# Flamingo layer, one core: the values' product and the output projection one step later, all middle probabilities turned by VectorE

## What is computed

```python
q = rmsnorm(layernorm(x) @ Wq.T)            # 32 heads of 128
k, v = rmsnorm(ctx @ Wk.T), ctx @ Wv.T      # 8 heads of 128, 4 query heads share one
probs = softmax(q @ k.T / sqrt(128) + mask) # 64 x 64 for each sequence and head
x = x + tanh(g_xattn) * ((probs @ v) @ Wo.T)
x = x + tanh(g_ffn) * experts_and_shared(layernorm(x))
```

## Time and profile before

| what | value |
|---|---|
| median of 3 launches (lowest, highest) | 1366.54 us (1366.28, 1366.75) |
| the profiled execution: device time | 1367.91 us |
| the profiled execution: span of the core | 1366.2 us |
| TensorE busy | 1351.8 us, 99% |
| VectorE busy | 1041.6 us, 76% |
| ScalarE busy | 505.4 us, 37% |
| GpSimd busy | 359.9 us, 26% |
| mean granted TensorE clock | 0.999 |

### The profile page before, as it was taken

One profiled execution on the slowest core, in us unless ns is written; L12 is line 12 of the kernel. 1 busy time (PEld: TensorE's weight loads), 2 busy tenths in 40 slices (PEclk: granted clock), 3 DMA queues, 4 the chain that ended last, 5 costly groups with the idle time before them and its releaser, 6 DMA issues.

```text
span 1366.2 us, 24589 instructions
## 1 busy us (share of the span) xinstructions
PE 1351.8 (99%) x8473; PEld 1092.8 (80%) x8474; DVE 1041.6 (76%) x2190; ACT 505.4 (37%) x1085; POOL 359.9 (26%) x375
## 2 busy tenths in 40 slices
PE   8999999999999999999999999999999999999998
PEld 7888877888888888888888888888887888777777
DVE  6676668898888888898988888888687655334459
ACT  4233244343434444344334343434344321222242
POOL 1122232212121221212121212122112100467746
PEclk9999999999999999999999999999999999999999
DMA  6766631222122221222121222212222344555548
GB/s 208 248 190 204 187 112 40 59 56 72 50 57 66 62 59 47 76 53 59 50 78 48 59 63 66 55 51 59 55 78 85 132 171 161 193 185 162 168 158 297
DMA packets 178209, 146.13 MB, mean 107 GB/s; under 512 B 77376, under 2 KB 139328, under 8 KB 177856
## 3 DMA queue, kind: packets, MB, share of 16 engines
q1 hardware_dynamic: 170592, 120.17, 29.4%
q0 software_dynamic: 7520, 24.65, 5.4%
HBM read 97.06 MB, written 47.71 MB: 106 GB/s over the span
## 4 chain that ended last, share of the span: by engine, by line
PE 80%; DVE 3%; issue 1%; DMA 0%; ACT 0%; POOL 0%; DVEq 0%; ACTq 0%
PE ps L677 20%; PE ps L679 19%; PE ps L678 19%; PE ps L1071 6%; PE ps L761 5%; PE ps L808 4%; PE ps L1087 3%; PE ps L1066 2%; PE ps L793 1%; DVE acc L2086 1%; DVE acc L2093 1%; PE ps L984 1%; PE ps L816 0%; PE ps L1118 0%; PE ps L769 0%
## 5 line engine op out<-in xcount | busy, mean ns | idle before, releaser
L574 POOL CAST vth<-vt 128x256 fp32r<-128x256 f32 x64 | 25.4, 397 | 538.6 <-PE ps L808 536.6
L1268 ACT CAST ah<-ps 128x256 fp32r<-128x256 f32 x256 | 83.1, 381 | 208.4 <-PE ps L679 202.0
L677 PE MATMUL ps<-hT,w0h 128*128 128x512 f32 x384 | 152.2, 396 | 1.2 <-DVE w0l L1542 1.2
L679 PE MATMUL ps<-hT,w0h 128*128 128x512 f32 x384 | 149.8, 390 | 0.0
L678 PE MATMUL ps<-hT,w0l 128*128 128x512 f32 x384 | 149.6, 390 | 0.0
L568 POOL TENSOR_TENSOR qr<-qv,mhalf 128x8 f32<-128x8 f32 x64 | 105.1, 1642 | 139.2 <-DVE qv L1672 113.5
L1228 ACT ACTIVATE qs<-ps,wqk 128x512 f32<-128x512 f32 x128 | 88.2, 689 | 125.8 <-PE ps L679 125.8
L1623 DVE TENSOR_TENSOR acc<-ps,acc 128x512 f32<-128x512 f32 x128 | 88.0, 687 | 50.5 <-PE ps L679 50.3
L677 PE MATMUL ps<-w0l,ah 128*128 128x512 f32 x256 | 105.9, 414 | 0.0
L1241 ACT ACTIVATE pb<-pb 128x256 f32<-128x256 f32 x128 | 48.3, 419 | 154.4 <-DVE pb L1692 154.4
L677 PE MATMUL ps<-w1l,ah 128*128 128x512 f32 x256 | 105.1, 411 | 0.0
(11 more groups left out here) (255 smaller groups left out, 3172.8 us busy)
## 6 DMA issues: line engine op xcount, KB each, us to landing
wraw<-in_w_att SPq DMA_DIRECT2D x64, 256.0 KB, 2.7
vbuf<-vo SPq DMA_DIRECT2D x16, 512.0 KB, 3.3
kbuf<-ko SPq DMA_DIRECT2D x16, 512.0 KB, 5.3
kt<-kbuf SPq DMA_DIRECT2D x128, 64.0 KB, 2.2
vt<-vbuf SPq DMA_DIRECT2D x64, 128.0 KB, 2.2
wgu<-in_w_gu SPq DMA_DIRECT2D x4, 2048.0 KB, 7.9
y<-ybuf SPq DMA_DIRECT2D x16, 512.0 KB, 6.9
pbuf<-pbT SPq DMA_DIRECT2D x26, 256.0 KB, 2.0
```

Source lines behind the costliest of these rows:

```text
L677: pe.matmul(dst, l_hi, r_lo, start=first, stop=False)
L679: return pe.matmul(dst, l_hi, r_hi, start=False, stop=last)
L1268: act.copy(ah[:, bp, :, b2, :], pv_view(bp, b2)).then_inc(a_hi, 1)
```

## The change

- The values' product and both halves of the output projection come one step later: TensorE's step i now handles index i-2 (`probs_v(i - 2)`, `project_out` of i-3 and i-2), and ScalarE's and VectorE's parts for them move with it (`a_hi_tile(i - 2)`, `a_rest(i - 2)`, `add_out(2 * i - 3)`).
- The probabilities of all steps 2 to 56 take VectorE's transposition and the way over `pbuf`. TensorE's transposes remain at steps 0, 1 and 57 to 63. The rounding and the subtraction of an even step come one step later, those of an odd step at the end of its own step.
- At step 56 (`catch_up`) both index 54 and index 55 are handled, and from step 57 on the old order stands (`last_step`).
- The query sums of step 3 go through `q_sums` in place of `add_quarters` (`TURNED`).
- GpSimd's split of the values comes one step later, behind the inverse root of the step before.
- SyncE's loop is written out: in every middle step the store of `pbT` (`probs_out`) comes first, in odd steps then `load_k`, weight slice, `probs_back`, values; in even steps `probs_back`, values, weight slice.
- The low part of an odd weight slice stays last in VectorE's odd step, that of an even slice stays between the two turned squares of the odd step.

```diff
@@ -50,8 +50,8 @@
 NC = T // CT
 CB = CT // S
 STEPS = KVH * NC
-BY_DMA = (4, STEPS - NC)
-TURNED = (3, STEPS - NC + 1)
+BY_DMA = (2, STEPS - NC + 1)
+TURNED = (4, STEPS - NC + 1)
 E, EI = 16, 128
...
-            def next_loads(d, odd, x_tiles=(), k=None):
-
-                i = 2 * d + odd
-                if k is not None:
-                    sp.wait_ge(p_turned, k + 1)
-                    sp.wait_ge(p_back, 64 * k + 64)
-                    sp.dma_start(pbuf, pbT[:].rearrange("p c m i -> p c (m i)")).then_inc(p_out, 16)
-                if odd:
-                    sp.wait_ge(s_done, i + 1)
-                    load_k(d + 1)
...
-                    sp.wait_ge(v_split, 2 * i + 2)
-                    sp.dma_start(vt[:].rearrange("p b t -> p (b t)"), vbuf[i + 1]).then_inc(vt_in, 16)
+            def load_v(j):
+                sp.wait_ge(v_split, 2 * j)
+                sp.dma_start(vt[:].rearrange("p b t -> p (b t)"), vbuf[j]).then_inc(vt_in, 16)
+
+            def load_slice(i):
                 sp.wait_ge(w_hi, i + 8)
                 sp.wait_ge(w_lo, i + 8)
                 sp.dma_start(wraw[:], w_att[i + NC]).then_inc(wr_in, 16)
-                for n in x_tiles:
+
+            def probs_out(i):
+                sp.wait_ge(p_turned, i - BY_DMA[0] + 1)
+                if i > BY_DMA[0]:
+                    sp.wait_ge(p_back, 64 * (i - BY_DMA[0]))
+                sp.dma_start(pbuf, pbT[:].rearrange("p c m i -> p c (m i)")).then_inc(p_out, 16)
+
+            def probs_back(i):
+                sp.wait_ge(p_out, 16 * (i - BY_DMA[0] + 1))
+                sp.wait_ge(pT_evac, 2 * i)
+                for c in range(4):
+                    sp.dma_start(pt_raw[32 * c:32 * c + 32].rearrange("p q m i -> p q (m i)"),
+                                 p_ld[c]).then_inc(p_back, 16)
...
+            for i in range(STEPS - NC + 1):
+                if by_dma(i):
+                    probs_out(i)
+                if i % 2:
+                    sp.wait_ge(s_done, i + 1)
+                    load_k(i // 2 + 1)
+                if i == 0:
+                    load_v(1)
+                if i % 2 or not by_dma(i):
+                    load_slice(i)
+                if by_dma(i):
+                    probs_back(i)
+                    load_v(i)
+                if i % 2 == 0 and by_dma(i):
+                    load_slice(i)
+            load_v(STEPS - NC + 1)
+
+            for t in range(1, NC - 1):
+                i = STEPS - NC + t
+                if t % 2:
+                    sp.wait_ge(s_done, i + 1)
+                    load_k(i // 2 + 1)
...
             split_v(1)
-            split_v(2)
-            with pool.Fori(3, STEPS - 2) as j:
+            inverse_root(3)
+            with pool.Fori(4, STEPS - NC + 2) as j:
+                split_v(j - 2)
+                inverse_root(j)
+            split_v(STEPS - NC)
+            split_v(STEPS - NC + 1)
...
+            def next_query(i):
+                if i % NC == NC - 1:
+                    pe.wait_ge(w_lo, i + 5)
+                for h in range(2):
+                    pe.wait_ge(q_sq, 2 * i + 1 + h)
+                    q_head(h, (i + 1) % 2, (i + 1) % NC // 2, att(i + 1)).then_inc(q_done, 1)
+
+            def step(i):
+
+                next_query(i)
+                probs_v(i - 2, i % 2)
+                scores((i + 1) // 2, (i + 1) % 2)
+                pe.wait_ge(acc_done, 2 * (i - 2) + 1)
+                project_out(1, att(i - 3), (0, 1))
+                if i + 1 == TURNED[0]:
+                    pe.wait_ge(const_dve, 6)
+                add_quarters(i + 1)
+                project_out(1, att(i - 3), (2, 3))
+                if i % NC == 2:
+                    pe.wait_ge(w_lo, i + 6)
+                projected_0(i - 2, att(i - 2))
+
...
+            def catch_up(i):
+
+                next_query(i)
+                probs_v(i - 2, 0)
+                scores((i + 1) // 2, (i + 1) % 2)
+                q_sums(i + 1)
+                pe.wait_ge(acc_done, 2 * (i - 2) + 1)
+                project_out(1, att(i - 3), (0, 1, 2, 3))
+                projected_0(i - 2, att(i - 2))
+                probs_v(i - 1, 1)
+                pe.wait_ge(acc_done, 2 * (i - 1) + 1)
+                project_out(1, att(i - 2), (0, 1, 2, 3))
+                projected_0(i - 1, att(i - 1))
+
...
-                probs_v(1, 1)
                 pe.wait_ge(s_scaled, 3)
                 pe.wait_ge(ss_turned, 3)
...
-                pe.wait_ge(const_dve, 6)
-                pe.wait_ge(acc_done, 4)
-                transpose_probs(2, 0)
-                outputs(1, W[0], W[0])
-                step(1, 1, 2, W[0], W[0], W[0])
-
...
-            group((STEPS - NC) // 2, 1, last=True)
+                q_sums(3)
+
+            opening()
+            for i in range(3, STEPS - NC):
+                step(i)
+            catch_up(STEPS - NC)
+            for i in range(STEPS - NC + 1, STEPS - 1):
+                last_step(i, o_ready=STEPS if i == STEPS - NC + 1 else None, last=(i == STEPS - 2))
 
             r = STEPS - 2
...
+            def probs_hi(i, odd, bank=2):
+                if by_dma(i):
+                    act.wait_ge(p_back, 64 * (i - BY_DMA[0] + 1))
+                    act.wait_ge(pv_done, 2 * i + 2 - 2 * odd)
+                    act.copy(raw_view(0, odd), pt_raw[:]).then_inc(pT_hi, 2)
...
+            def act_step(i):
+
+                queries(i)
+                a_hi_tile(i - 2, 0)
+                if i % 2:
+                    probs_hi(i - 1, 0)
+                a_hi_tile(i - 2, 1)
+                split_slice(i, att(i + NC), i % NC)
+                if i % 2:
+                    probs_hi(i, 1)
+                exps(i + 1)
+
...
             def probs_lo(i, odd, bank=2):
-                if odd:
+                if by_dma(i):
+                    dve.wait_ge(pT_hi, 2 * i + 2)
+                    dve.tensor_tensor(raw_view(1, odd), pt_raw[:], raw_view(0, odd), ALU.subtract).then_inc(pT_evac, 2)
...
+            def turn_probs(i):
+                dve.wait_ge(p_ready, 2 * i + 2)
+                if i > BY_DMA[0]:
+                    dve.wait_ge(p_out, 16 * (i - BY_DMA[0]))
+                dve.transpose(pbT[:].rearrange("p c m i -> p (c m i)"),
+                              pb[:].rearrange("p (m z) (h j) -> p (z h) m j", z=2, h=2)).then_inc(p_turned, 1)
+
+            def dve_step(i):
+
+                odd = i % 2
+                turn_probs(i)
+                turn_squares(i + 1, 0)
+                sum_squares(i + 1, 0)
+                if odd:
+                    slice_lo(i - 1, att(i + NC), i % NC - 1)
+                turn_squares(i + 1, 1)
+                sum_squares(i + 1, 1)
+                split_sums(i + 1)
+                a_rest(i - 2, 0)
+
+                def while_root():
+                    if odd:
+                        probs_lo(i - 1, 0)
+                    add_out(2 * i - 3, 1, (2 * i - 5) % NT)
+                    a_rest(i - 2, 1)
+
+                def while_exp():
+                    add_out(2 * i - 2, 0, (2 * i - 4) % NT)
+
+                softmax(i + 1, while_root, while_exp, turn_before=i - BY_DMA[0] + 1)
                 if odd:
                     probs_lo(i, 1)
...
+                    slice_lo(i, att(i + NC), i % NC)
+
+            def dve_catch_up(i):
+
+                turn_probs(i)
+                a_rest(i - 2, 0)
+
+                def while_root():
+                    add_out(2 * i - 3, 1, (2 * i - 5) % NT)
+                    a_rest(i - 2, 1)
+
+                def while_exp():
+                    add_out(2 * i - 2, 0, (2 * i - 4) % NT)
+
+                softmax(i + 1, while_root, while_exp, turn_before=i - BY_DMA[0] + 1)
+                slice_lo(i, att(i + NC), i % NC)
+                a_rest(i - 1, 0)
+                add_out(2 * i - 1, 1, (2 * i - 3) % NT)
+                a_rest(i - 1, 1)
+                probs_lo(i, 0)
+                add_out(2 * i, 0, (2 * i - 2) % NT)
```

More of the change, by code:

```diff
@@ L305, in rows_by_pe, with by_dma, pT_before, att @@
             return isinstance(n, int) and (n < 2 or n == NT - 1)
[L307 to L317, removed]
+        def by_dma(i):
+            return BY_DMA[0] <= i < BY_DMA[1]
+        def pT_before(i):
+            return i if i < BY_DMA[0] else i - (BY_DMA[1] - BY_DMA[0])
+        def att(r):
+            return W[r // NC % 2]
+        def raw_view(x_, odd):
+            return pt[x_][:, :, odd * P:odd * P + P].rearrange("p m (q i) -> p q m i", q=4)
         def turned(j):
@@ L434, in next_loads @@
                     sp.dma_start(xt3[n % 2][:], x[n]).then_inc(x3_in[n % 2], 16)
[L435 to L458, removed]
+                load_v(i + 1)
             def store_h2(n):
@@ L826, in gate_up_half, with projected_0 @@
                     mm.then_inc(gu_done, 1)
[L828 to L837, removed]
+            def projected_0(r, w_o):
                 pe.wait_ge(a_hi, 4 * r + 6)
@@ L841, in outputs @@
                 project_out(0, w_o, (0, 1, 2, 3))
[L843 to L848, removed]
```

(52 more changed lines are left out.)

143 lines of the change are left out of this document (41 added, 102 removed).

## The result

| | median us | lowest, highest | launches |
|---|---|---|---|
| before | 1366.41 | 1365.63, 1366.75 | 4 |
| after | 1493.02 | 1492.11, 1493.88 | 4 |

The ratio is 1.0927, with a 95% interval of 1.0908 to 1.0946: slower by 127 us. The prediction had said 1437 with a range of 1421 to 1470, so the direction was right and the time too low by 56 us. The profiled execution of after took 1492.87 us, with a span of 1491.1.

What follows compares the result with a forecast made beforehand. TensorE, 99% busy, was taken as the bound, so delays reaching it cost full length. -13.0 +72.8 +2.6 -0.6 +7.6 +1.5 = +70.9 us on 1367.9 gives 1438.8, as launch median 1437 us; range 1421 to 1470.

Steps and rivals of the forecast that it cites:

- The transposes, -0.48 us each time: TensorE's steps without transposes: each four removed save 0.48 us, the difference of two neighbouring steps; -13.0 us in the sum.
- the rival with 18 us: TensorE's transposes cost their durations, 1.1 us for four: 18 us lower, 1419 us; chance 0.05.
- The keys behind a wait, 26 x 2.8 = +72.8 us: SyncE's odd steps: key loads queue behind the store awaiting VectorE's transposition, so TensorE waits 2.8 us before the scores.
- The clock, "I take no fall there": TensorE behind each odd step's 2.8 us wait: no clock fall after 26 us of dense work, 0 us.
- The rival stood there: TensorE's clock falls behind each wait: 0 to 39 us more, 1440 to 1476 us; chance 0.25.
- The way back and the split sums, +2.6 and 0: Odd steps: late return of probabilities delays VectorE, 0.1 x 26 = 2.6 us; VectorE's later split sum of squares costs 0.
- The bound for the first (8 us): Upper bound for the probabilities' way back in odd steps: 8 us, where 2.6 was taken.
- the bound of 0.1 a pair for the second: Upper bound for VectorE's late split sum of squares: 0.1 us a pair, where 0 was taken.
- The even steps' slice, "hidden with over 1 us to spare": Even steps: weight slice lands by 12.6 us, its rounding precedes the exponentials at 14.60, so no cost.
- Ends, -0.6 and +7.6: Both ends: scores after step 3's wait at 238.3 against 238.88, -0.6 us; step 56 takes back moved work, +7.6 us.
- "nearly 7": TensorE's idle time in step 3, nearly 7 us, with a clock fall behind it counted once as +1.5 us.
- The "faster" rival: SyncE's odd-step queue: keys come in time, TensorE stays the bound, 1354 us; chance 0.05.

Runs made afterwards that it cites:

- k_rests: `k_hi` with the odd slice's low part moved into VectorE's root wait of the next even step, and even slices rounded behind the exponentials: 1361.12 us.
- k_first_turns: `k_first` plus four TensorE transposes of an identity, read by nobody, ahead of the values' product in each odd step: 1379.55 us.
- k_first: The changed kernel with SyncE issuing an odd step's four key loads ahead of the store of the turned probabilities: 1371.72 us.
- fill6: The changed kernel with six useless matmuls of 512 columns ahead of the odd steps' scores: 1449.25 us.
- fill3: The changed kernel with three useless matmuls of 512 columns ahead of the odd steps' scores: 1476.03 us in one launch.
- k_hi: `k_first` with ScalarE rounding an odd step's returned probabilities behind the next exponentials, not ahead of them: 1366.26 us.
- k_slice: `k_first` with an even step's weight slice loaded ahead of the four loads of the probabilities, not behind them: 1369.65 us.

## Why the prediction was wrong

- **The transposes, -0.48 us each time.** Right in size on TensorE: 0.45 a pair in `k_rests`. In `k_first_turns` they cost 0.18 a pair, 0.29 by the medians, since VectorE hides a part. The durations as a price (the rival with 18 us) are refuted by both. The sentence from the Trainium skill's page "TensorE: Matmul & The Clock Gate", Part 4, gives a duration; taken as time on the path it would have been off by a factor of over two.
- **The keys behind a wait, 26 x 2.8 = +72.8 us.** Right: 75.4, 2.90 each. The worked step from the softmax's end over transposition, store and loads to the scores has 5.33 us, and 5.41 is the mean in after, measured from the transposition's start. That is partly luck, for two of its parts were off and cancelled: the first key load follows the store by 0.37 us, not 0.67, and from its issue to the scores it is 4.3 us, not 3.8. `k_first` shows that it is the order in the queue and not the loads.
- **The clock, "I take no fall there".** This is the step that failed. Each of the 26 waits lowered the clock, at 1.5 us each in 21 cases and 2.7 us in five: 45 us where the sum had 0. The rival stood there, with chance 0.25 and a bound of 1.5 each (39 us in all), and was what happened; even its top, 1476, was 17 us too low, because five falls cost more than its bound and other terms were short too. The argument against it was that over 26 us of dense matmuls lay between the waits, and that in the earlier trace rows the gaps lay close together. No row of before had a lone gap of this length, so the dense work around it was an argument without a row. The rows that were there (gaps of 1.16 and 1.94 us, clock 0.83) spoke for the fall, and the runs agree with them: gaps like the first did nothing in `fill6`, and the second lies where the clock starts to fall in `fill3`.
- **The way back and the split sums, +2.6 and 0.** Under-sized. From an even step's scores to the next odd step's it is 427.3 us in the 26 pairs of after. TensorE's own work is 26 x 13.22 = 343.7 of them and the wait for the keys 75.4; 8.1 are left, 0.31 a pair. Some 1.8 of these belong to the keys' wait, since the last matmul ahead of it has nothing to overlap with (from it to the scores it is 3.18 us, of which 2.90 are idle; 0.21 in before). The other 6.3 are at the even step's fold: in six steps a wait for the split sums that is listed (2.5 us, above), in the others mostly one too brief for the list (between 300 and 900 us the fold's weight load waited in all 19, 8.6 us in all). Without the keys' wait the lateness is 26.95 - 26.49 = 0.46 a pair (12 us), presumably since VectorE then gets no pause from TensorE's wait. In `k_first` it had two parts: the rounding ahead of the exponentials (5.5 us, `k_hi`) and the rest of the odd slice at the end of its step, with the even slice's rounding ahead of the exponentials (5.1 us together, `k_rests`). The bound for the first (8 us) held it, the bound of 0.1 a pair for the second was half of what it took.
- **The even steps' slice, "hidden with over 1 us to spare".** Wrong, at little cost. It had the keys' landing, 2.2 us, and in the pair shown it came 4 us after its issue. ScalarE waited for it in each of the 19 even steps between 300 and 900 us of after (two lines, since the weights have two buffers):

```profile
ACT w0h L1299 <- DMA wraw<-in_w_att: 24.8, 11, 4.0
ACT w1h L1299 <- DMA wraw<-in_w_att: 17.1, 8, 2.9
```

In that pair its rounding starts 14.3 us into the even step, and the softmax ends 17.3 us into it, 17.1 before: little of ScalarE's waiting reached it. What it costs with the keys late was not run; with the keys first, `k_slice` puts the price at about 2 us.

- **Ends, -0.6 and +7.6.** Right: scores of step 4 at 238.3 as worked out, catch-up step +7.7. The 8.1 us of idle time in step 3 ("nearly 7") lowered the clock as well: 15.5 us from its scores to the next, 2.3 above 13.22, for which the sum had 1.5.
- **The "faster" rival** fell: the keys do not come in time. With its condition met by hand, `k_first` gave 1372 and not 1354, because the rival left out the second and third thing that were late (12 us) and had 1 to 2 us for both ends, where the catch-up step alone costs 7.7.

From the scores of step 4 to those of step 57 the prediction's terms give 778.0 us (713.6 - 26 x 0.48 + 72.8 + 2.6 + 1.5), and 831.4 were measured, 53.4 more. Of these the clock makes 45.8 (45 behind the 26 waits and 2.3 behind step 3's, against 1.5), lateness 3.7 (6.3 against 2.6), the keys 4.4 (75.4 + 1.8 against 72.8), and TensorE's own work is 0.5 shorter (53 x 13.22 us against 701.1): 53.4. Ahead of and behind this stretch it is 0.6 more. The last 2 us of the 56 are the launches: the median of after lies 0.15 above its profiled execution, that of before had lain 1.4 below.

## What to carry to other kernels

A wait placed at the head of an in-order DMA queue delays all loads behind it: for every queue list what is issued behind the new wait and when its reader needs it, and issue first what needs no wait. Where TensorE will idle for 2 us or more in such a kernel, add the clock to the price of the wait (here 1.5 to 2.7 us on top of 2.9), and if the wait can't go, shortening it below the point where the clock falls gains more than its length. And where one wait hides slack on the other engines, taking it away brings the next lateness out: three reorderings were needed, and only with all of them did the 0.45 us a pair show that the change was made for.

## What was not expected of the hardware

- A lone gap of TensorE of 2.07 us or more between long stretches of matmuls at 2.4 GHz was followed by matmuls at 1.2 GHz every time (11 in `fill3`, 26 in after); gaps up to 1.68 us never (8 in `fill3`, 24 in `fill6`); between 1.70 and 2.00 it went either way (five of seven in `fill3` fell, and neither of the two in `fill6`, 1.72 and 1.76). Which of two equal gaps costs 1.5 us and which 2.7 stays open: the gaps of the five expensive cases of after are 2.72, 2.87, 3.06, 3.21 and 3.90, and other gaps of 2.7 to 3.3 us were cheap.
- 12 useless matmuls in 26 steps made the kernel 41 us faster. They ran in time in which TensorE had idled, and kept the clock at 2.4 GHz behind it.
